# Eight tiles instead of two in one iteration of the expert loop

## What is computed

```python
logits = h @ router_weight.T + router_bias          # 8 experts
top_vals, top_idx = jax.lax.top_k(logits, 2)
top_w = jax.nn.softmax(top_vals, axis=-1)
...
gate_up = jnp.einsum('th,ehj->etj', h, gate_up_proj) + gate_up_proj_bias[:, None, :]
gate, up = gate_up[..., ::2], gate_up[..., 1::2]
gate = jnp.minimum(gate, 7.0)
up = jnp.clip(up, -7.0, 7.0)
act = (up + 1.0) * (gate * jax.nn.sigmoid(gate * 1.702))
expert_out = jnp.einsum('eti,eih->eth', act, down_proj) + down_proj_bias[:, None, :]
out = jnp.einsum('te,eth->th', scores, expert_out)
...
x = x + s * silu(out)                               # s: the attention's output
```

## Time and profile before

| | us |
|---|---|
| median of three runs | 1115.05 (1113.02 to 1116.56) |
| the profiled execution | 1113.86 |
| its span, first to last instruction | 1112.0 |
| PE busy | 941.5 (85%) |
| DVE busy | 938.0 (84%) |
| ACT busy | 776.8 (70%) |
| POOL busy | 221.7 (20%) |

### The profile page before, as it was taken

How to read it: one execution, slowest core, us unless ns; L and a number is a source line. 1 busy time by engine, 2 the same in 40 slices (tenths; PEclk the granted TensorE clock), 3 DMA queues, 4 the chain that set the end, 5 groups by cost and what they waited for, 6 DMA issues and landing times. The chain is left out here.

```text
span 1112.0 us, 25771 instructions
## 1 busy us (share of the span) xinstructions
PE 941.5 (85%) x6626; PEld 659.5 (59%) x6627; DVE 938.0 (84%) x1873; ACT 776.8 (70%) x1982; POOL 221.7 (20%) x427
## 2 busy tenths in 40 slices
PE   5999858989889998988999898858999999962665
PEld 4787645666666666666666666644555555532544
DVE  6778688999999999999999999935777777754987
ACT  3554438999999999999999999942333333325663
POOL 2000001222222232222322232210000000017771
PEclk9999987999999999999999999988999999996677
DMA  7999986676786767757575665402222222223553
GB/s 258 377 366 370 328 318 137 172 183 149 172 199 165 175 157 187 184 128 165 120 159 130 139 151 128 95 15 66 80 84 77 85 80 80 80 94 96 174 182 107
DMA packets 92410, 178.11 MB, mean 160 GB/s; under 512 B 11744, under 2 KB 50144, under 8 KB 91360
## 3 DMA queue, kind: packets, MB, share of 16 engines
q1 hardware_dynamic: 74336, 147.38, 49.1%
q0 software_dynamic: 7680, 20.98, 6.5%
q10 hardware_dynamic: 10368, 9.44, 2.5%
HBM read 108.56 MB, written 69.21 MB: 160 GB/s over the span
## 5 line engine op out<-in xcount | busy, mean ns | idle before, releaser
L1050 DVE TENSOR_REDUCE nmax<-bank 128x1 f32<-128x1024 f32 (+3 forms) x256 | 260.4, 1017 | 4.0 <-PE bank L882 4.0
L983 ACT ACTIVATE Pr_long<-bank,nmax 128x1024 f32<-128x1024 f32 (+3 forms) x256 | 252.0, 984 | 12.2 <-DVE nmax L1050 12.1
L1010 ACT COPY AT<-bank 128x512 f32<-128x512 f32 (+3 forms) x384 | 177.0, 493 | 4.4 <-PE bank L921 2.5
L880 PE MATMUL bank<-Ks_first,Qs_first 128*128 128x512 f32 (+3 forms) x384 | 124.1, 413 | 31.1 <-ACT Pr_short L997 19.8
L1242 PE MATMUL bank<-gu_sb,xsT 128*128 x288 | 140.7, 612 | 4.8 <-DVE hid L1359 0.5
L997 ACT ACTIVATE Pr_short<-bank,nmax 128x128 f32<-128x128 f32 (+3 forms) x256 | 138.3, 540 | 8.9 <-DVE nmax L1068 1.6
L921 PE MATMUL bank<-ident,Pr_long 128*128 128x128 f32 x832 | 127.9, 281 | 18.1 <-DVE Pr_long L1100 18.1
L1100 DVE SCALAR_TENSOR_TENSOR Pr_long<-Pr_long,coef 128x1024 f32<-128x1024 f32 (+3 forms) x128 | 137.6, 1075 | 0.0
L880 PE MATMUL bank<-Ks_second,Qs_second 128*128 128x512 f32 (+3 forms) x384 | 119.4, 400 | 18.7 <-ACT Pr_short L997 18.4
L882 PE MATMUL bank<-maskb,identb 128*128 128x128 bf16 x512 | 118.1, 233 | 0.0
L921 PEld LDWEIGHTS bank<-ident,Pr_long 128*128 128x128 f32 x832 | 90.8, 143 | 31.7 <-issue 27.6
(11 more groups left out here) (147 smaller groups left out, 1647.0 us busy)
## 6 DMA issues: line engine op xcount, KB each, us to landing
q_parts<-PARTS SPq DMA_DIRECT2D x32, 512.0 KB, 5.9
k_parts<-PARTS SPq DMA_DIRECT2D x32, 512.0 KB, 5.9
Qs_first<-q_parts SPq DMA_DIRECT2D x64, 256.0 KB, 6.2
Ks_first<-k_parts SPq DMA_DIRECT2D x64, 256.0 KB, 7.1
Qs_second<-q_parts SPq DMA_DIRECT2D x64, 256.0 KB, 5.9
Ks_second<-k_parts SPq DMA_DIRECT2D x64, 256.0 KB, 6.7
xs_dram<-zeros SPq DMA_DIRECT2D x8, 1152.0 KB, 8.4
xs<-xs_dram SPq DMA_DIRECT2D x72, 128.0 KB, 2.0
```

Source lines behind the costliest of these rows:

```text
L880: nc.tensor.matmul(at[:, c0:c1], Qs[head][:, m, q * P:(q + 1) * P], Ks[head][:, m, c0:c1], start=True, stop=(c1 < N))
L983: nc.scalar.activation(long_probs(p)[:, m, 0:N], long_slot[m][:, 0:N], ACT.Exp, bias=nmax[:, 4 * p + m:4 * p + m + 1], scale=1.0, accum_ou ...
L1010: nc.scalar.copy(AT[u % 6][:, 0:w], tb[u % BANKS][:, 0:w]).then_inc(unit_out, 1)
L1050: nc.vector.tensor_reduce(nmax[:, 4 * p + m:4 * p + m + 1], long_slot[m][:, 0:N], AX.X, ALU.max, negate=True).then_inc(long_maxed, 1)
```

## The change

The constant BLOCK = 8 is the number of tiles in one iteration. The table expert_rows has 9 rows of 10 numbers instead of 36 rows of 4: eight experts of the block and the first two of the next. It is built with the same three instructions in the first stage. The loader fills ten registers at once. run_steps makes step 0 ahead as before, then a loop of 8 iterations with eight steps each, and eight steps behind the loop. The steps themselves, their order, the buffers and the semaphores are the same; the number of a tile is now made of four times the counter.

```diff
+BLOCK = 8
...
-        expert_rows = sb("expert_rows", [P, SLOT_TILES // 2, 4], I32)
+        expert_rows = sb("expert_rows", [P, SLOT_TILES // BLOCK, BLOCK + 2], I32)
...
-                    pairs = cmp[:, SLOT_TILES * E:SLOT_TILES * (E + 1)].rearrange("p (i u) -> p i u", u=2)
-                    NR = SLOT_TILES // 2
-                    nc.vector.tensor_scalar(expert_rows[:, :, 0:2], pairs, float(E - 1), None, ALU.min)
-                    nc.vector.tensor_scalar(expert_rows[:, 0:NR - 1, 2:4], pairs[:, 1:], float(E - 1), None, ALU.min)
-                    then(nc.vector.memset(expert_rows[:, NR - 1:NR, 2:4], 0))
+                    pairs = cmp[:, SLOT_TILES * E:SLOT_TILES * (E + 1)].rearrange("p (i u) -> p i u", u=BLOCK)
+                    NR = SLOT_TILES // BLOCK
+                    nc.vector.tensor_scalar(expert_rows[:, :, 0:BLOCK], pairs, float(E - 1), None, ALU.min)
+                    nc.vector.tensor_scalar(expert_rows[:, 0:NR - 1, BLOCK:], pairs[:, 1:, 0:2], float(E - 1), None, ALU.min)
+                    then(nc.vector.memset(expert_rows[:, NR - 1:NR, BLOCK:], 0))
...
-                    registers = [eng.alloc_register(f"expert{n}") for n in range(4)]
+                    registers = [eng.alloc_register(f"expert{n}") for n in range(BLOCK + 2)]
...
-                    load = load or (lambda it: None)
+                    load = load or (lambda j: None)
                     step(0, 0, load(0))
-                    with eng.Fori(0, NIT3 - 2) as it:
-                        e = load(it)
-                        step(it, 1, e)
-                        step(it, 2, e)
-                    e = load(NIT3 - 2)
-                    for n in (1, 2, 3, 4):
-                        step(NIT3 - 2, n, e)
+                    last = SLOT_TILES // BLOCK - 1
+                    with eng.Fori(0, last) as j:
+                        e = load(j)
+                        for n in range(1, BLOCK + 1):
+                            step(j * (BLOCK // 2), n, e)
+                    e = load(last)
+                    for n in range(1, BLOCK + 1):
+                        step(last * (BLOCK // 2), n, e)
```

## The result

| | before | after |
|---|---|---|
| median of the runs | 1115.05 us (1113.02 to 1116.56) | 1121.33 us (1119.88 to 1122.69) |
| profiled execution, and its span | 1113.86 us, 1112.0 us | 1121.33 us, 1119.5 us |
| instructions | 25771 | 25279 |
| first to last L1242 (after: L1245) of the expert stage | 753.26 to 984.49, 231.2 us | 752.81 to 990.03, 237.2 us |
| idle time of TensorE ahead of that line, by the page | 4.8 us | 14.3 us |

The change made the kernel slower by about 0.6%: ratio 1.0057, interval 1.0040 to 1.0074. The forecast was 1108.0 us, with a range of 1103.5 to 1111.5, so the time lies outside it and on the other side.

A forecast was written before the change was run, and what follows sets the result against it. TensorE was taken to bound the expert stage, with holes at the back edges. Removing 26 gave -10.1 us, longer loads +3.0, sum -7.1: from 1115.05 to 1108.0 us, range 1103.5 to 1111.5.

The forecast's parts named there:

- What bounds the kernel: Expert stage: TensorE's matmul stream bounds it, with an excess of 0.439 us per two-tile iteration at the back edge.
- whom the hole belongs to: Loop's back edge: branch 208 ns, arithmetic 59, load 333 together stall TensorE's queue; each of 26 removed gives 0.39 us.
- The 0.05 us left in: Part of the excess, ahead of act_in's transposes: late ys, put to a store wait, stays; otherwise 1.3 us more gained.
- the mean of 3.05: Steps inside the eight-tile body: 3.02 and 3.07 us in turn, 3.05 in the mean.
- a load of ten: Loads at stage start, loop entry, back edges and exit: ten registers cost 0.30 us more each, 3.0 us over ten loads.
- Rival (b): Register load: ten cost more than in proportion, say 1.0 us each, 6.7 us lost, time 1111.7 us; chance 0.07.
- The rule against the change: Register loads: about 200 ns per register, 12 us over ten loads, so 1.9 us slower than now; the prediction disagreed.
- Rival (a): Steps without a back edge: VectorE or ScalarE becomes the bound, steps 3.10 to 3.14 us, time 1111 to 1113.5; chance 0.11.
- Rival (c): Back edges: the longer body's code must be fetched after each jump; at 2 us each the time is 1122; chance 0.04.
- Rival (d): Expert loop: the excess belongs to the alternation of two buffers, so nothing changes, 1115 us; chance 0.04.
- The bounds it named: Wrong if body steps exceed 3.07 us, the load 0.83, or the first instruction after a taken branch comes over 0.5 later.

The follow-up runs named there:

- Experiment 5: The kernel before (loop of two tiles) without the register load inside the loop: 1099.73 us, ratio 0.9852.
- experiment 6: The changed kernel (loop of eight tiles) without the register load inside the loop: 1102.53 us, ratio 0.9887.
- experiment 7: The kernel before, with the load in the loop on TensorE alone, 1110.57 us, or on VectorE alone, 1101.36 us.
- experiment 1: The kernel before with 27 loads of 1 to 16 registers added on TensorE ahead of the expert stage, from three table words: 1156.73 us, one run.

## Why the prediction was wrong, point by point

**What bounds the kernel.** Right: the stage is TensorE's, and every second step had a hole at the back edge. Its size, 0.44 us, was right too. Experiment 5 puts the stage without the holes at 215.4 us against 231.2.

**The step that failed first: whom the hole belongs to.** The prediction added branch, register arithmetic and load to 0.60 us "in which the queue hands out no matmul", and let 0.4 of it show. So it counted a fixed price for each back edge, of which the load was one part, and took each back edge that went as 0.39 us gained. Without the load the hole is 0.00 (experiments 5 and 6): the branch and the arithmetic are covered. With TensorE's load alone it is 0.33, the length of that load, and with VectorE's alone 0.05 (experiment 7). What was removed was 26 loads of one access each, and what was added is paid by the access.

**The 0.05 us left in.** It was put down to a wait on an earlier store and the work ahead. The trace has that store landed 1.7 us after its issue, and its buffer is written again 6 us after. It belongs to VectorE's load: no steps of 3.07 in the changed kernel except the second one behind a back edge, 0.05 in each pair with VectorE's load alone (experiment 7). The steps inside the body were 3.02, better than the mean of 3.05 that was forecast, and so the 26 x 0.05 = 1.3 us that the sum had left out of the gain came as well.

**The term that was mis-sized: a load of ten.** Taken as 0.63 us, bounded by 0.333 and 0.83 "if all were per register". The upper bound was none: it rested on one length only, and on that length being four times something. It was one access. On the boundary ten words are 1.08 us, off it 2.40 (2.67 at the back edges). Dear as they are, these loads stand where nothing covers them. The back edges by the forecast would have cost 7 x 0.74 = 5.2 us. Loads of 1.08 in place of 0.63 make it 7 x 1.07 = 7.5, so 2.3 more; the four off the boundary add 4 x 1.59 = 6.4; the half clock at three of them adds 3 x 1.64 = 4.9 (1.53, 1.69 and 1.69 from L1245 to L1245). Together 18.8, and 18.9 was read, 13.7 over the forecast. The whole stage was 13.1 over it (7.1 us shorter by the forecast, 6.0 longer as measured): the 1.3 us above go off, 0.35 come on at entry and exit (1.25 in place of three times 0.30), and some 0.4 is left unassigned. The clock had no term in the sum at all; without it the kernel would still have been about 1 us slower than before.

**Rival (b)** had the mechanism and, for the loads on the boundary, the size: "say as three loads of four, 1.0 us", 1111.7 us. The table with rows of 48 bytes is that kernel, at 1111.8, 4.0 us under the kernel before that was measured with it. By the prediction's terms with the measured load and the 1.3 us above that is 10.1 + 1.3 - 10 x 0.75 = 3.9. Its limit, "at 1.33 us a load the gain is gone", becomes 1.47 with them, an estimate; the mean of the changed kernel's loads at its back edges is 1.99. What it lacked was the boundary and the clock.

**The rule against the change.** The prediction set the page's 200 ns a register ("Runtime: NRT & Kernel Launch", section "Instruction fetch mechanics", of the Trainium skill) against "at most 0.083" of the trace, and dismissed it. Word by word the chip takes 0.233 us a register from SBUF (experiment 1), so the rule was near the truth for 4 of the 7 loads, and its estimate, 1.9 us slower, had the right sign. That is in part luck: from the boundary ten words cost 0.108 each, half the rule, and most of the 6 us is the clock, of which it says nothing. The row on which it was dismissed measured one access of four words.

**Rival (a)** did not happen: VectorE and ScalarE keep up with 3.02 us a step. **Rival (c)**, slower by fetching the body's code, gave nearly the right time, 1122, for a reason that is not there: with the loads out, the body of eight runs across its back edges at 3.02 us (experiment 6), and the branch on PE's queue takes at most 211 ns, as before:

```profile
L1214 PEldq COMPARE_BRANCH  x8: 76/207/211, 785.2 to 973.3; - x8
```

**Rival (d)**, that the excess belongs to the alternation of the buffers, is refuted by the steps of 3.02 inside the body.

**The bounds it named.** "I am wrong if ... the load is over 0.83": it was, and that is how it was wrong. The first instruction behind a branch came late only because the load stood there.

## What to carry to other kernels

A cost read at one length is a price for that length only: before multiplying it, find a row at a second length, or take the whole of it, per unit, as the bound. Register loads from a table should begin on 16 bytes, with rows of a multiple of four words, even if some of them are not used; and they should stand where the engine's queue has work in hand. TensorE's load alone cost 9.2 us more at the head of the loop of two than behind the matmuls (1110.57 against 1101.39), and with both engines' loads moved inside the body the loop of eight came 16.1 us under the kernel before. Such a place has to be sought on each engine: ahead of ys VectorE's load still held up the stage. Look at what is left of a hole when each of its parts alone is taken away, before paying for fewer of all of them.

## What the runs showed of the hardware that I had not expected

- A load into registers from SBUF: about 0.08 us once, 0.25 for each aligned group of four words, about 0.235 for each word outside such groups. Off a 16-byte boundary there are no groups, even where the middle of the row is aligned (8 words from word 1: 1.93 us; from word 0: 0.59).
- Two engines' loads at the same time do not slow one another by that alone: 2.41 us beside 2.29, and 1.08 beside 1.07. At back edges loads were longer all the same (2.64 to 2.68 instead of 2.41, 1.25 to 1.33 instead of 1.08), and why is open.
- After TensorE had stood still for 2.1 to 2.4 us between stretches of full work, the granted clock was 0.50 for about 3 us in 8 of 18 cases at back edges, 1.5 to 1.7 us of lost time each; after 0.7 to 0.8 us in none of 43. Why these eight is not settled.
- A taken branch of 208 ns and 59 ns of register arithmetic on TensorE's queue cost its array nothing, 33 times over.
